# Merged probability products, keys' blocks kept in idle operands, and reciprocals spread by a transfer, in a post-norm transformer layer

## The reference

```python
qkv = x @ Wqkv + bqkv                                   # 16 heads of 16 channels
att = einsum('bhqd,bhkd->bhqk', q, k) * scale
att = softmax(where(causal, att, -inf), axis=-1)
y = einsum('bhqk,bhkd->bhqd', att, v) @ Wout + bout
x = layernorm(x + y)
tlin = lambda x, w, s: einsum('bsi,oi->bso', x, w) * s  # w holds multiples of whole numbers
h = silu(tlin(x, w1_w, w1_s)) * tlin(x, w2_w, w2_s)     # 256 -> 1024
h = gelu(tlin(h, h1_w, h1_s))                           # 1024 -> 1024
h = gelu(tlin(h, h2_w, h2_s))                           # 1024 -> 1024
x = layernorm(x + tlin(h, w3_w, w3_s))                  # 1024 -> 256
```

## Time and profile before

| | us |
|---|---|
| median of 3 runs | 2323.64 |
| lowest and highest run | 2322.57, 2328.25 |
| profiled execution | 2323.13 |
| its span in the trace | 2321.4 |

### The profile page before, as it was taken

The page is one execution under the profiler, slowest core; times in us unless marked ns, Lnnn a source line. Parts: engine busy times, 40 slices in busy tenths (PEclk is TensorE's granted clock), DMA queues, the critical chain, the costliest instruction groups (busy, mean ns, idle before and its releaser), DMA issues.

```text
span 2321.4 us, 52007 instructions
## 1 busy us (share of the span) xinstructions
PE 2208.8 (95%) x16294; PEld 1871.2 (81%) x16294; DVE 1278.9 (55%) x3961; ACT 1293.6 (56%) x2769; POOL 488.1 (21%) x896
## 2 busy tenths in 40 slices
PE   4758999999999999999999999999999999999998
PEld 2336888888888888888888888888888888888898
DVE  4564565555556556555655556565555656555433
ACT  1334566565656656565665656656565565656543
POOL 1121222122222212212221222212122221222211
PEclk7779999999999999999999999999999999999999
DMA  8642223232232323223232232323223232312000
GB/s 288 209 142 63 66 59 74 55 76 60 63 71 59 75 55 71 65 61 71 61 75 55 67 69 61 70 61 75 55 61 75 59 69 64 75 42 50 23 6 10
DMA packets 96838, 166.18 MB, mean 72 GB/s; under 512 B 21568, under 2 KB 40768, under 8 KB 96576
## 3 DMA queue, kind: packets, MB, share of 16 engines
q1 hardware_dynamic: 88736, 139.02, 25.9%
q10 hardware_dynamic: 7840, 23.86, 3.0%
HBM read 93.08 MB, written 71.83 MB: 71 GB/s over the span
## 4 chain that ended last, share of the span: by engine, by line
PE 77%; DMA 4%; issue 3%; SPq 3%; ACT 2%; DVE 2%; POOL 0%; ACTq 0%; DVEq 0%; POOLq 0%
PE ring L1055 38%; PE ring L1041 8%; PE pM L951 6%; PE pO L973 6%; PE pS L939 6%; PE ring L1068 5%; PE ring L985 4%; PE ring L1021 2%; DMA dn<-den_d 2%; DMA qk_d<-c 2%; PE ring L1005 1%; SPq L504 1%; DVE full_g L805 1%; PE ring L959 1%; ACT L698 1%
## 5 line engine op out<-in xcount | busy, mean ns | idle before, releaser
L766 DVE CUSTOM_DVE_ANT_0 pM<-pM,mask 128x512 f32<-128x512 f32 (+3 forms) x1024 | 493.4, 507 | 318.7 <-PE pM L951 262.5
L1055 PE MATMUL ring<-Xhi,H 128*128 128x256 f32 x2048 | 515.4, 291 | 6.6 <-ACT full_h L711 5.0
L1055 PE MATMUL ring<-Yhi,H 128*128 128x256 f32 x2048 | 507.4, 285 | 0.0
L1055 PE MATMUL ring<-Ylo,H 128*128 128x256 f32 x2048 | 502.8, 283 | 0.0
L1055 PE MATMUL ring<-Xlo,H 128*128 128x256 f32 x2048 | 499.3, 282 | 0.0
L1055 PEld LDWEIGHTS ring<-Xhi,H 128*128 128x128 f32 x2048 | 391.1, 191 | 18.7 <-ACT full_h L711 11.7
L1055 PEld LDWEIGHTS ring<-Ylo,H 128*128 128x128 f32 x2048 | 390.9, 191 | 3.2
L1055 PEld LDWEIGHTS ring<-Xlo,H 128*128 128x128 f32 x2048 | 392.1, 191 | 1.1
L1055 PEld LDWEIGHTS ring<-Yhi,H 128*128 128x128 f32 x2048 | 390.2, 191 | 2.6
L951 PE MATMUL pM<-Ks,Qs 128*128 128x512 f32 x992 | 297.4, 358 | 48.4 <-DMA Ks<-qk_d 31.4
L710 ACT ACTIVATE Yhi<-ring,cols 128x256 fp32r<-128x256 f32 x256 | 120.8, 472 | 285.8 <-PE ring L1055 251.2
(11 more groups left out here) (102 smaller groups left out, 3336.8 us busy)
## 6 DMA issues: line engine op xcount, KB each, us to landing
qk_d<-c SPq DMA_DIRECT2D x124, 256.0 KB, 3.4
Qs<-qk_d SPq DMA_DIRECT2D x124, 192.0 KB, 4.4
Ks<-qk_d SPq DMA_DIRECT2D x124, 192.0 KB, 4.9
qk_d<-c SPq DMA_DIRECT2D x124, 128.0 KB, 3.1
xTs<-in_xT SPq DMA_DIRECT2D x16, 512.0 KB, 4.4
raw<-in_h ACTq DMA_DIRECT2D x8, 1024.0 KB, 24.5
xz<-in_x SPq DMA_DIRECT2D x16, 512.0 KB, 6.5
Oc<-Osb SPq DMA_DIRECT2D x256, 32.0 KB
```

What stands on the lines that cost most here:

```text
L766: nc.vector.tensor_tensor_reduce(pM[:, h % 2, 0:n], pM[:, h % 2, 0:n], mask[:, T - n:T], 1.0, NEG, ALU.add, ALU.max, mx[:, t, h:h + 1]).th ...
L1055: mm = nc.tensor.matmul(to, w, x_part, start=(k == 0 and m == 0), stop=(k == KB - 1 and m == 1))
```

## The change

- **One run of products a group.** Key blocks 2 and 3 get places of their own: for even groups in the idle part of `Xlo`, for odd ones in that of `Ylo` (operands of the feed-forward products). `pv` becomes one step a group (`pv:..:1`) with all sixteen products, put into the Gelu stage behind its exponentials. In iteration 0 the first batch keeps two runs a group.
- **Denominators spread by transfer.** The reciprocals are stored once, unsplit, and two DMAs read each head's row 16 times, straight into 128 partitions of `rec`, which now lies over the buffer `c`. VectorE multiplies from there. The selection matrix, TensorE's two products and the split are gone; `qk` waits on ScalarE until `rec` has been read.
- **Orders.** All three tables are new. Iteration 0 now also holds `y`, `ln1` and `x1_turn` of batch 0, all exponentials and products of group 0 of batch 1 and the maxima of its group 1; a step `hold` makes ScalarE's queue wait for a stack before it issues more weight copies. The first stretch of iteration 1 shrinks to the branch. On all engines but TensorE the loop's seam moves to the step TURN in the first Gelu stage.

```diff
-table:0:Exp:4 qk:1:0 exp:0:2:0 exp:0:2:1 h2:-1:0:0:0 max:0:3:3:0 h2:-1:0:0:1 exp:0:2:2 exp:0:2:3 h2:-1:0:1:0
-max:0:3:3:1 exp:0:2:4 exp:0:2:5 h2:-1:0:1:1 exp:0:2:6 exp:0:2:7 max:0:3:3:2 max:0:3:3:3 pv:0:2:0 max:0:3:2:0
-exp:0:2:8 max:0:3:2:1 exp:0:2:9 max:0:3:2:2 pv:0:2:1 max:0:3:2:3 exp:0:2:10 h2:-1:0:2:0 h2:-1:0:2:1
-h_act:-1:h2:0:0 pv:0:2:2
...
-table:0:Gelu:5 pv:0:2:3 o_out:0:2 stack:1:0 h_act:-1:h2:0:1 h_rest:-1:h2:0:0 h_act:-1:h2:0:2 max:0:3:1:0
...
+table:0:Exp:4 qk:1:0 exp:0:2:0 exp:0:2:1 h2:-1:0:0:0 h2:-1:0:0:1 exp:0:2:2 exp:0:2:3 max:0:3:3:0 h2:-1:0:1:0
+max:0:3:3:1 exp:0:2:4 exp:0:2:5 max:0:3:3:2 h2:-1:0:1:1 exp:0:2:6 max:0:3:3:3 exp:0:2:7 max:0:3:2:0 exp:0:2:8
+h2:-1:0:2:0 max:0:3:2:1 exp:0:2:9 max:0:3:2:2 exp:0:2:10 h2:-1:0:2:1 max:0:3:2:3 h_act:-1:h2:0:0
+
+table:0:Gelu:5 stack:1:0 h_act:-1:h2:0:1 h_rest:-1:h2:0:0 pv:0:2:1 o_out:0:2 h_act:-1:h2:0:2 max:0:3:1:0
...
+TURN = 1 + STEPS.index(("h_act", -2, ("h2", 1, 2)))
...
+        done = FIRST + [(kind, off - 1, a) for kind, off, a in HEAD]
+        return FIRST + [s for s in steps if s not in done]
+    return steps
...
+        def small_probs(at, name):
+
+            at += 2 * HALF * 4
+            return (over(nc, at, f"probs_{name}2", [P, PAIRS, 2, T // 2], F32),
+                    over(nc, at + PAIRS * T * 4, f"probs_{name}3", [P, PAIRS, 2, P], F32))
...
+        probs_y = small_probs(ylo_at, "y")
...
+        rec = over(nc, c_at, "rec", [P, CB, T], F32)
...
-        def probs_of(kt, p):
-            return (probs_b if kt % 2 else probs_a)[:, p]
+        def probs_of(steps, off, g, kt):
+
+            if kt < 2:
+                return (probs_a, probs_b)[kt]
+            if steps is HEAD and off == 0:
+                return probs_a[:, :, :, 0:T // 2] if kt == 2 else probs_a[:, :, :, T // 2:T // 2 + P]
+            small_x, small_y = (probs_x, probs_y)
+            return (small_y if g % 2 else small_x)[kt - 2]
+
+        def pv_runs(steps, off):
+            return 2 if steps is HEAD and off == 0 else 1
...
                     elif kind == "rec_save":
-                        sp.wait_ge(rc_done, (b + 1) * 3)
-                        sp.dma_start(rec_d.rearrange("a h (c n) -> (h c) a n", n=H * T // P), rc[:].bitcast(F32)).then_inc(rec_saved, 16)
+                        sp.wait_ge(rc_done, b + 1)
+                        sp.dma_start(rec_d.rearrange("h (c n) -> (h c) n", n=H * T // P), dn[:]).then_inc(rec_saved, 16)
                     elif kind == "rec_load":
                         sp.wait_ge(rec_saved, (b + 1) * 16)
-                        sp.dma_start(rec[2 * H:4 * H].bitcast(F32), rec_d.rearrange("a h n -> (a h) n")).then_inc(rec_in, 16)
+                        rows = rec_d.rearrange("(m h) (a n) -> m h a n", m=CB, a=1).broadcast_to([CB, H // CB, D, T])
+                        for m in range(CB):
+                            sp.dma_start(rec[:, m], rows[m]).then_inc(rec_in, 16)
...
+                    elif kind == "hold":
+
+                        act.wait_ge(*stack_landed(steps, off, b, a[0]))
...
-                        need(act, pv_done, b * (NG * TB) + g * TB + kt - 1)
+                        need(act, pv_done, (b * NG + g) * 2 + (kt > 1 and pv_runs(steps, off) > 1))
...
+                        if not (steps is HEAD and off == 0):
+                            need(act, o_norm, (b - off) * CB + CB * normed_before(g))
...
-                        dve.wait_ge(rc_done, b * 3 + 1)
-                        nc.vector.tensor_copy(rc[:, 0], dn[:]).then_inc(rc_done, 1)
-                        dve.wait_ge(rc_done, b * 3 + 2)
-                        nc.vector.tensor_tensor(rc[:, 1], dn[:], rc[:, 0].bitcast(F32), ALU.subtract).then_inc(rc_done, 1)
                     elif kind == "den_turn":
+                        dve.wait_ge(rec_in, (b + 1) * (16 * CB))
                         for m in range(CB):
-                            dve.wait_ge(r_ready, b * CB + m + 1)
-                            nc.vector.tensor_tensor(Oc[:, m], Oc[:, m], ring[:, BANKS[kind, off, (m,)]],
-                                                    ALU.mult).then_inc(o_norm, 1)
+                            nc.vector.tensor_tensor(Oc[:, m], Oc[:, m], rec[:, m], ALU.mult).then_inc(o_norm, 1)
...
-                        g, kt = a
-                        n = e_cols(kt)
-                        if kt == 0:
+                        g, last = a
+                        runs = pv_runs(steps, off)
+                        if runs == 1 or not last:
                             if g == 0:
                                 pe.wait_ge(v_copied, (b + 1) * TB)
                             need(pe, o_out, b * NG + g)
-                        pe.wait_ge(mask_done, b * (NG * TB * PAIRS) + e_of(g, kt, PAIRS - 1) + 1)
-                        for p in range(PAIRS):
-                            for s in range(2):
-                                j = 2 * p + s
-                                mm = nc.tensor.matmul(pO[32 * j:32 * j + VW, kt * P:T], Vo[:, kt, G * g + j],
-                                                      probs_of(kt, p)[:, s, 0:n],
-                                                      start=(kt == 0), stop=(kt == TB - 1))
-                        mm.then_inc(pv_done, 1)
+                        for kt in range(TB) if runs == 1 else range(1, TB) if last else (0,):
+                            n = e_cols(kt)
+                            pe.wait_ge(mask_done, b * (NG * TB * PAIRS) + e_of(g, kt, PAIRS - 1) + 1)
+                            for p in range(PAIRS):
+                                for s in range(2):
+                                    j = 2 * p + s
+                                    mm = nc.tensor.matmul(pO[32 * j:32 * j + VW, kt * P:T], Vo[:, kt, G * g + j],
+                                                          probs_of(steps, off, g, kt)[:, p, s, 0:n],
+                                                          start=(kt == 0), stop=(kt == TB - 1))
+                        mm.then_inc(pv_done, 2 // runs)
...
-                    elif kind == "den_turn":
-
-                        pe.wait_ge(rec_in, (b + 1) * 16)
-                        for m in range(CB):
-                            to = bank(kind, off, (m,))
-                            nc.tensor.matmul(to, sel[2 * H:4 * H, m], rec[2 * H:4 * H], start=True, stop=True).then_inc(r_ready, 1)
```

More of the change, by code:

```diff
@@ L73 @@
[L73 to L77 removed]
+table:0:Exp:0 y:-1:0:0 y:-1:0:1 max:0:1:3:0 y:-1:1:0 h2:-2:1:0:0 exp:0:0:2 exp:0:0:3 y:-1:1:1 max:0:1:3:1
@@ L141 @@
[L141 to L145 removed]
+table:0:Exp:0 table:0:Gelu:1 table:0:Exp:2 weight_flag:0
@@ L173, in ring_banks @@
     for kind, off, args in plan_steps:
-        if kind == "den_turn":
-            keys = [(kind, off, (m,)) for m in range(CB)]
-        elif kind in ("qk", "v", "gu", "x1_turn", "neg_max", "bias", "weight_flag") or kind in PARTED:
+        if kind in ("qk", "v", "gu", "x1_turn", "neg_max", "bias", "weight_flag") or kind in PARTED:
             keys = [bank_of(kind, off, args)]
@@ L201, in gated_before, with normed_before @@
     return sum(s[0] == "ffn_hi" for s in STEPS[:at])
+def normed_before(g):
+    at = next(n for n, s in enumerate(STEPS) if s[0] == "qk" and s[2] == (g,))
+    return sum(s[0] == "den_turn" for s in STEPS[:at])
 def steps_of(i):
@@ L208, in steps_of @@
     steps = [s for s in STEPS if i is None or 0 <= i + s[1] < B]
-    return FIRST + [s for s in steps if s not in FIRST] if i == 1 else steps
+    if i == 1:
+        done = FIRST + [(kind, off - 1, a) for kind, off, a in HEAD]
+        return FIRST + [s for s in steps if s not in done]
+    return steps
 def banks_of(steps):
@@ L341, in build @@
         SAVES = 16 * 4
-        N_CONSTS = 10
+        N_CONSTS = 7
         def need(eng, s, n):
@@ L545, in _ @@
                                     pattern=[[-1, P]], channel_multiplier=1).then_inc(consts, 1)
-            for n in range(2):
-                pool.wait_ge(consts, 8 + n)
-                nc.gpsimd.affine_select(out=heads, in_=heads, compare_op=ALU.not_equal, fill=1.0, base=-n * H,
-                                        pattern=[[-1, H], [0, D]], channel_multiplier=1).then_inc(consts, 1)
             pool.wait_ge(consts, N_CONSTS)
```

134 lines of the change are left out of this document (62 added, 72 removed).

## The result

The changed kernel takes 2283.88 us (median of 4 runs, 2280.26 to 2287.90); the kernel before, timed beside it, 2323.22. The ratio is 0.9828, 95% interval 0.9817 to 0.9840: 39 us faster. The profiled execution took 2284.5 us, its span is 2282.7.

What follows compares the result with a forecast made beforehand. TensorE's stream was taken to bound the steady three quarters, waits the first 200 us. Steady gain 27.9 + 15.0 - 6 = 36.9, start 17, sum 53.9 off 2323.1: 2269 us; own range 2259 to 2282, with neighbours 2247 to 2297.

Steps and rivals of the forecast that it cites:

- Steady part: Batches after the start: 27.9 from junctions, 15.0 from the denominators' turn, less 6 for the transfer, a gain of 36.9 us.
- Start: Stretch up to the first feed-forward: it ends at 178.1 instead of 195.2 us, a gain of 17, bounds 5 to 27.
- a first `gu` product behind 190 us: Sign against the forecast, in the start: the first `gu` product was expected near 173 us; behind 190 made it wrong.
- the half-the-engines rival: Loads of the reciprocals: 8 of 16 DMA engines carry them, TensorE waits 1.3 us, 14 us more, 2283; chance 0.22.
- The junctions: Entering and leaving a run of probability products on TensorE: 0.21 us each, nine fewer a batch, 27.9 us gained.
- The turn of the denominators: TensorE's two products that turned the reciprocals: removal gains 1.0 us (0.82 to 1.09) a batch, 15.0 in 15 batches.
- The split: Two VectorE operations on the reciprocals: their removal and the larger store go against each other and count nothing.
- The transfer's wait: Output projection behind the reciprocals' load: TensorE waits 0 to 0.9 us a batch, taken as 0.4, 6 us in 15 batches.
- The cover: Exp stages: moving about 2 us of products out of each costs nothing, as TensorE's stream stays 3.3 us above ScalarE.
- The cover rival: Four Exp stages: the moved products were cover, TensorE waits for ScalarE, +5.9 us a batch, 2389 in all; chance 0.05.
- First keys: Start: the first stacked keys land at about 28.8 us instead of 36.56, with the other weight copies made to wait.
- the way of the negated maxima: Start: negated maxima pass through ScalarE and four DMAs in TensorE's path, allowed 8 us in all.

Runs made afterwards that it cites:

- all three edits: Changed kernel with third group's low key half written before the second norm, batch 1's negated maxima issued before the reciprocals' store, and all weight tests moved forward: 2267.04 us, 0.9758.

## Why the prediction was right, and where its steps were not

The direction (faster) and the range (2247 to 2297) held; the number, 2269, was 15 us too low, outside the forecast's own 2259 to 2282 by 2 us. Steady part: 36.9 us forecast; 33.6 in thirteen periods and 1.8 behind them. The period is 133.6, as forecast (133.5), but by luck, as shown below. Start: 17 forecast, 3.3 measured. That is the step that failed: the forecast itself had named a first `gu` product behind 190 us as a sign of being wrong, and it came at 196.38. That the time is the 2283 of the half-the-engines rival is a coincidence: its 14 us were to be a longer wait at the projection, and what is missing is at the start.

**The junctions** were mis-sized. In sums from start to start over thirteen batches, 13 runs a batch cost, with what they add before and behind, 13.17 us before and 10.02 after: 3.15 us for nine junctions, 0.35 each, not 0.21. The part not seen was the product behind a run (0.10).

**The turn of the denominators** was a little low, for the same reason. The two products take 1.00 us a batch from start to start, before and when they were put back, but entering costs 0.09 more (970.32 to 970.53 in the earlier trace rows, 0.21 instead of 0.12) and the product behind them 0.10 (the next starts at 971.75, 0.22 behind the one at 971.53): 1.19 in all, where the forecast took 1.0 and at most 1.09.

**The split** was counted as nothing, since VectorE is idle half the time. It stood between two maxima for which TensorE waits, and its removal brought about 0.6 us a batch (the intervals of the last query block's maxima go from 2.18 to 1.55; 0.5 came when it was put back).

**The transfer's wait** was forecast as 0.4 us at the projection. There it is small (a recorded 0.9 us in thirteen batches, by the intervals ahead of the projection up to 0.17 a batch); at the bank that VectorE frees later it is 0.84 a batch. I had named what stands behind the waiting multiplication and had called it slack. The half-the-engines rival had the mechanism (8 in flight, 16 when the outer size is 16) and the wrong price: the multiplication starts 5.2 us behind the first issue (4.6 behind the second, from which the forecast had taken 4.4 to 6.6), as 256 packets of 84 ns by eights are 2.7 us for both loads together, and most of the rest is there for any load (1.8 us for the small one of the earlier trace rows).

**The cover** was put at nothing because the fourth stage had 3.3 us more of TensorE than of ScalarE. A stage's sum doesn't tell. Take out of the period the probability products with their junctions, the selection products, the split and the projection's intervals (13.17 + 1.19 + 0.63 + 2.89 before, 10.02 + 3.73 after, 11.43 + 3.73 with block 0 back between the exponentials): 118.3 us remain before, 119.8 after, 118.8 with block 0 back. So 1.5 us a batch were lost elsewhere; 1.0 of it is shown by the experiment to be cover, the rest is what the sum leaves, and no run shows that it is cover too. The cover rival had the right mechanism, at a sixth of its price.

So a batch: 3.15 + 1.19 + 0.63 - 0.84 - 1.5 = 2.6 us, measured 2.58; the last term is the remainder, so the agreement proves nothing by itself. The forecast's 2.5 came from terms whose errors cancelled: 1.9 + 1.0 - 0.4.

**The start.** First keys at 28.4, as forecast (28.8). From there, 121 instead of 107 to the last group's products: the way of the negated maxima through ScalarE and four DMAs was allowed 8 us and held TensorE for 5.29 + 5.93 + 7.29 = 18.5, and the rest of the pace from the first keys on was 3.9 longer. From the products to the reciprocals' multiplication 20.7 (21.5 forecast), so it starts at 141.6, not 128.6. From there I had allowed 49.5 us; as the projection of batch 1 moved by 3.3, the start is worth 191.9 where 195.2 stood, 50.3 behind the multiplication. Thirteen of the missing 14 us lie before it. That such a wait is worth its length doesn't follow: with the negated maxima first the last of them shrank by 8 us and the median time didn't change. Which chain bounds 142 to 196 us isn't settled. VectorE is busy 32.5 of the 40 us from 143 to 183; TensorE's granted clock over the whole stretch is 0.62 where it was 0.82 before, and was 0.67 with the negated maxima first and 0.68 with all three edits. No run separates the two, and the clock had no term in the forecast. The starts of kernels with the same first part scatter by about 2.5 us (batch 1's projection at 289.9 to 292.5, the first `gu` product at 193.8 to 196.4), so smaller effects are open.

## What to carry to other kernels

Price a removed junction or wait by the intervals from start to start of both neighbours, the product behind the run included. Price a wait that you add on an in-order engine not at the instruction that waits but at the first later one whose result somebody needs: here the transfer was nearly free at its reader and cost 0.84 us at a bank freed behind it, and exchanging two steps gave that back (12 us). And "the stage has enough other work" doesn't show cover: look at the gaps between the pairs that must answer each other.
